# A semaphore increment on GpSimd behind every row gather of a graph network kernel

## The chip, the cores and the metric

The kernel runs on one core of one Trainium2 chip, as one launch of a hand-scheduled program with five instruction streams. The metric is device time in microseconds (us); lower is better. Three runs of the kernel before gave 9662.51, 9666.22 and 9667.9 us.

## What is computed

The reference is a two-part graph network on 12,500 nodes of 96 features and 200,000 edges, sorted by destination (cut to what matters):

```
h = relu(layernorm(x))                       # x: (12500, 96)
neigh1 = segment_sum(h[src], dst) * inv_deg
neigh2 = segment_sum(neigh1[src], dst) * inv_deg
x = x + 0.5 * neigh1 + 0.5 * neigh2
h = relu(layernorm(x))
for W_msg, W_edge, W_root, b in layer 1, layer 2:
    msg = h[src] @ W_msg + edge_attr @ W_edge            # (200000, 96)
    h = leaky_relu(max over the edges of a node (msg) + h @ W_root + b)
return x + h
```

So four times, one after the other, a row of 96 floats is fetched for each of the 200,000 edges and folded into the rows of the destination nodes: twice as a sum, twice as a maximum.

## The kernel before, in words

**Rounds.** The program has four rounds (`ROUNDS`, r = 0 to 3). In a round GpSimd gathers the rows of table r from HBM for all edges; rounds 0 and 1 sum (`sums`), rounds 2 and 3 take maxima (`maxima`). After the gathers a node stage works through the nodes in 14 chunks (`CHUNKS`) and writes the next table, and the next round's gathers wait until that table is stored (`tstored`, line 367).

**Groups.** 512 edges (4 columns of 128) are a group; there are 391 groups (`GROUPS`) a round. A group takes four gathers, one for each column: `pool.indirect_dma_start` at line 374 fetches 128 rows of 384 bytes, one for each partition, and its DMA adds 16 to the semaphore `landed` of the group's slot. That is 1564 gathers a round and 6256 in all. The rows go into `rows`, a ring of 8 group slots (`RING`). Before the first gather of group g, from the ninth group on, GpSimd waits until TensorE has used the slot: `pool.wait_ge(used, g - RING + 1)`, where `used` is `picked` in the sum rounds and `rows_ps` in the maximum rounds. Both are counters that TensorE increments with its last matmul of a group. GpSimd's program is written out in full; nothing else stands between the gathers of a round.

**Who uses the rows.** In the sum rounds TensorE multiplies the rows of a group with one-hot matrices (line 557, 8 matmul instructions a group) and increments `picked`; VectorE waits for `picked`, adds the windows into `comp` (line 784) and builds the next one-hots (lines 767 and 773); ScalarE waits for `picked` too in round 0 (line 435). TensorE waits for VectorE's folding of the group before the last one. In the maximum rounds TensorE adds the edge features and the rows in PSUM (lines 576 and 578) and increments `rows_ps`; VectorE scans (line 799); TensorE transposes the running maximum (line 589); ScalarE copies it (line 443); TensorE picks the segment ends (line 600) and ScalarE copies windows into `comp` (line 452). The edge features and the flags come by DMAs from SyncE's queue.

**The node stage on GpSimd.** Behind the gathers of a round GpSimd waits for the last folding and then builds some one-hots (line 388). Ahead of each chunk's one-hots it already has a semaphore increment of its own, `pool.sem_inc(pool_go, 1)` at line 386. No engine waits for `pool_go`.

Of the kernel before, what the change touches and what calls it, by code (L numbers as in the profile page):

```python
# [74 lines left out]
def after(q, n):  # L75

    return q >= n if known(q) else True


def pipeline(engine, body, lag):  # L80

    first = 2 + lag + (2 + lag) % 2
    pairs = (CHUNKS - first - 1) // 2
    for k in range(first):
        body(k, k % 2)
    with engine.Fori(0, pairs) as i:
        for s in range(2):
            body(i * 2 + (first + s), s)  # L90
    for k in range(first + 2 * pairs, CHUNKS + lag):
        body(k, k % 2)


def has(k, lag):

    return 0 <= k - lag < CHUNKS if known(k) else True


def gnn(nc, x, srcs, cur, prev, nxt, cur_r, prev_r, eat, wm1, we1, wr1, b1, wm2, we2, wr2, b2, out):  # L100
    with ExitStack() as ctx:
# [3 lines left out]
        def sem(name):  # L105
            return ctx.enter_context(nc.semaphore(name))
# [104 lines left out]
        pool_go, dve_go = sem("pool_goes_on"), sem("dve_goes_on")  # L211
# [132 lines left out]
        @block.gpsimd  # L344
        def _(pool):
            pool.memset(ident[:], 0.0).then_inc(const, 1)
            pool.memset(ident_b[:], 0.0).then_inc(const, 1)
            pool.memset(upto_b[:], 1.0).then_inc(const, 1)
            pool.memset(ones_b[:], 1.0).then_inc(const, 1)
            pool.wait_ge(const, 4)  # L350
            for eye in (ident, ident_b):
                pool.affine_select(out=eye[:], in_=eye[:], compare_op=ALU.not_equal, fill=1.0, base=0,
                                   pattern=[[-1, P]], channel_multiplier=1).then_inc(const, 1)
            pool.affine_select(out=upto_b[:], in_=upto_b[:], compare_op=ALU.is_ge, fill=0.0, base=0,
                               pattern=[[1, P]], channel_multiplier=-1).then_inc(const, 1)
            pool.wait_ge(const, 7)
            pool.affine_select(out=upto_b[:], in_=upto_b[:], compare_op=ALU.is_gt, fill=0.0, base=0,
                               pattern=[[0, P]], channel_multiplier=1).then_inc(const, 1)
            for to, w, step, first in ((iota_0, P, 1, 0), (iota_1, P, 1, 1), (iota_b, P, 1, 0), (tile_at, TILES, P, 0)):
                pool.iota(to[:], pattern=[[step, w]], base=first, channel_multiplier=0,  # L360
                          allow_small_or_imprecise_dtypes=True).then_inc(const, 1)
            pool.memset(comp[:], 0.0).then_inc(cleared, 1)

            pool.wait_ge(s_src, 16)
            for r in range(ROUNDS):
                for s in range(2):
                    pool.wait_ge(tstored[r][s], 16 * (CHUNKS // 2))
                used = picked[r] if r in sums else rows_ps[r]
                for g in range(GROUPS):
                    if g >= RING:  # L370
                        pool.wait_ge(used, g - RING + 1)
                    for j in range(GRP):
                        c = g * GRP + j
                        pool.indirect_dma_start(rows[:, g % RING, j, 0:D], None, tables[r][:, :],  # L374
                                                bass.IndirectOffsetOnAxis(src_sb[:, c:c + 1], 0)
                                                ).then_inc(landed[r][g % RING], 16)

                pool.wait_ge(folded[r], COLS)

                def spread(k, s):  # L380
                    if not has(k, 0):
                        return
                    pool.wait_ge(rel_ready[r], k + 1)
                    if after(k, 2):
                        pool.wait_ge(spread_ps[r], k - 1)
                    pool.sem_inc(pool_go, 1)
                    for j in range(POOL_HOTS[r]):
                        pool.tensor_scalar(spread_c[:, s, j, :], iota_1[:, :], rel_c[:, s, j:j + 1],  # L388
                                           None, ALU.is_equal).then_inc(spread_1h[r], 1)

                pipeline(pool, spread, 0)
# [587 lines left out]
```

## Time and profile before

| | |
|---|---|
| runs of the kernel before | 9662.51, 9666.22, 9667.9 us (median 9666.22) |
| the profiled execution's own time | 9629.93 us |
| its span, first to last instruction | 9628.2 us |
| GpSimd (POOL) busy | 6458.6 us, 67% of the span |
| of it the 6256 gathers | 6273.4 us |
| TensorE busy | 5576.1 us, 58% |
| VectorE busy | 3262.5 us, 34% |
| mean granted clock of TensorE | 0.648 of 2.4 GHz |
| DMA | 548.56 MB, mean 57 GB/s |

The profile is of one execution, which took 9629.93 us; the median of the runs lies 36.3 us above it. POOL is GpSimd, PE is TensorE's matmuls and PEld its weight loads, DVE is VectorE, ACT is ScalarE. A letter q behind an engine's name is its sequencer: instructions that only touch registers or semaphores. Those aren't counted as busy, and lists of instructions leave them out; the chain of waits shows them. "issue" is time in which an engine waited for nothing that the profile shows, "remote" a wait for a semaphore whose update could not be tied to an instruction.

### The profile page before, as it was taken

The page shows a single profiled execution, that of the slowest core. Times are in us where ns is not written, and L with a number is a line of the kernel's source. Part 1 is how long each engine was busy: PE and PEld are TensorE (multiplying, and loading weights), DVE is VectorE, ACT ScalarE, POOL GpSimd, SP SyncE. Part 2 cuts the span into 40 slices and gives each one's busy share as a digit, 9 for nine tenths or more (in the row PEclk, how much of TensorE's full clock was granted, in tenths as well). Part 3 has the DMA queues.
Part 4 walks back from the last instruction along what each step waited for, and adds up shares of the span by engine and source line. Part 5 has one row for each costly group of instructions (what it writes and reads, how often), then busy time and mean ns, then how long its engine had stood idle before and what let it go on. Part 6 is the DMA issues. An engine that isn't in the chain of part 4 may idle for free.

```text
span 9628.2 us, 100471 instructions
## 1 busy us (share of the span) xinstructions
PE 5576.1 (58%) x25651; PEld 4095.6 (43%) x25651; DVE 3262.5 (34%) x6693; ACT 1500.7 (16%) x5073; POOL 6458.6 (67%) x6525
## 2 busy tenths in 40 slices
PE   2333333334233333333578877878887887887888
PEld 1222222223222222222555555555564555555556
DVE  4333333334333232323423333333332333333334
ACT  1000000001000000000322222222232222222223
POOL 5666666664666666666566666766656666666665
PEclk6555555556555555555767777777786777677776
DMA  3111111111111111111133333333323333333332
GB/s 79 35 34 34 34 34 34 34 35 39 47 35 34 34 34 35 34 34 35 46 76 77 77 77 77 78 80 78 77 64 71 80 78 77 77 77 77 77 81 64
DMA packets 309643, 548.56 MB, mean 57 GB/s; under 512 B 183464, under 2 KB 183464, under 8 KB 284712
## 3 DMA queue, kind: packets, MB, share of 16 engines
q0 software_dynamic: 200192, 307.90, 16.3%
q1 hardware_dynamic: 108804, 239.50, 9.7%
q14 instruction: 77, 0.63, 0.0%
q8 instruction: 22, 0.36, 0.0%
q10 hardware_dynamic: 548, 0.17, 0.0%
HBM read 522.27 MB, written 24.87 MB: 57 GB/s over the span
## 4 chain that ended last, share of the span: by engine, by line
another core or an unknown queue 29%; PE 26%; issue 9%; DVE 8%; DVEq 2%; ACT 1%; ACTq 1%; POOL 0%; DMA 0%; POOLq 0%; SPq 0%
PE ps L578 7%; PE ps L576 6%; PE ps L600 6%; PE ps L589 3%; DVE arena L799 3%; DVE comp L784 3%; PE ps L557 2%; DVE arena L767 2%; DVEq L257 1%; DVEq L784 1%; PE ps L662 1%; PE ps L638 0%; ACTq L257 0%; PE ps L675 0%
## 5 line engine op out<-in xcount | busy, mean ns | idle before, releaser
L374 POOL DMA_INDIRECT rows<-table,src_sb x6256 | 6273.4, 1003 | 2930.3 <-issue 1767.5
L557 PE MATMUL ps<-arena,rows 128*98 128x128 f32 (+1 forms) x6256 | 1418.1, 399 | 2967.0 <-DVE comp L784 2634.6
L557 PEld LDWEIGHTS ps<-arena,rows 128*98 128x98 f32 (+1 forms) x6256 | 1179.5, 254 | 3226.7 <-DVE comp L784 2836.3
L799 DVE TENSOR_TENSOR_SCAN arena<-arena,ps 96x512 f32<-96x512 f32 x782 | 996.6, 1274 | 3238.6 <-remote 1989.8
L784 DVE TENSOR_TENSOR comp<-comp,ps 98x128 f32 (+1 forms) x3128 | 893.6, 286 | 2878.4 <-remote 2317.0
L578 PEld LDWEIGHTS ps<-ident,rows 128*96 128x96 f32 x6256 | 950.4, 208 | 912.9 <-issue 912.7
L600 PE MATMUL ps<-arena 128*96 128x128 f32 x6256 | 1180.2, 352 | 108.6 <-issue 72.4
L578 PE MATMUL ps<-ident,rows 128*96 128x128 f32 x6256 | 1173.3, 344 | 54.2 <-issue 53.4
L576 PE MATMUL ps<-arena,we 32*96 32x512 f32 x1564 | 1143.7, 819 | 27.3 <-DMA rows<-table,src_sb 27.3
L600 PEld LDWEIGHTS ps<-arena 128*96 128x96 f32 x6256 | 1052.2, 228 | 129.6 <-issue 124.4
L767 DVE TENSOR_TENSOR arena<-iota_b,meta 128x512 f32<-128x512 bf16 x1564 | 1053.0, 673 | 59.6 <-issue 55.1
L452 ACT COPY comp<-ps 96x128 f32 x3128 | 821.3, 263 | 1490.8 <-PE ps L600 573.6
L589 PE MATMUL ps<-ident,arena 96*128 96x96 f32 x3128 | 564.2, 322 | 757.8 <-DVE arena L799 653.8
L589 PEld LDWEIGHTS ps<-ident,arena 96*128 96x128 f32 x3128 | 449.1, 190 | 831.0 <-DVE arena L799 657.9
L443 ACT COPY arena<-ps 128x384 f32<-128x384 f32 x782 | 374.5, 479 | 1998.1 <-remote 1233.2
L435 ACT COPY rows<-root 128x4 f32 (+1 forms) x391 | 74.3, 197 | 2179.0 <-remote 1581.1
L492 ACT COPY rel_c<-node_rel 128x7 f32<-128x7 f32 (+1 forms) x42 | 8.5, 203 | 2261.8 <-DVE comp L784 2261.8
L388 POOL TENSOR_SCALAR arena<-iota,rel_c 128x128 f32<-128x128 f32 x252 | 172.0, 698 | 228.4 <-ACT rel_c L492 134.0
L576 PEld LDWEIGHTS ps<-arena,we 32*96 32x96 f32 x1564 | 236.2, 196 | 186.9 <-issue 125.4
L773 DVE TENSOR_TENSOR arena<-iota_b,meta 128x392 bf16<-128x392 bf16 x391 | 219.5, 561 | 12.0 <-issue 11.6
L563 PE MATMUL ps<-arena,ones_b 128*1 128x392 bf16 x391 | 168.3, 430 | 0.0
L662 PE MATMUL ps<-arena 128*128 128x96 f32 (+1 forms) x784 | 141.1, 354 | 6.4 <-ACT arena L504 4.8
(84 smaller groups left out, 1026.0 us busy)
## 6 DMA issues: line engine op xcount, KB each, us to landing
arena<-flags SPq DMA_DIRECT2D x194, 768.0 KB
rows<-table,src_sb POOLq DMA_INDIRECT x6256
arena<-in_eat SPq DMA_DIRECT2D x194, 256.0 KB
table<-arena SPq DMA_DIRECT2D x56, 336.0 KB, 2.7
out<-xs SPq DMA_DIRECT2D x13, 336.0 KB
xs<-in_x SPq DMA_DIRECT2D x6, 672.0 KB, 5.9
arena<-flags SPq DMA_DIRECT2D x2, 576.0 KB
src_sb<-in_srcs SPq DMA_DIRECT2D x1, 782.0 KB, 5.2
```

The costliest lines, as they stand in the source:

```text
L374: pool.indirect_dma_start(rows[:, g % RING, j, 0:D], None, tables[r][:, :], bass.IndirectOffsetOnAxis(src_sb[:, c:c + 1], 0)).then_inc(lan ...
L443: act.copy(runT[:, slot % SCANS].rearrange("p k d -> p (k d)"), ps[:, RUNT + slot % 2 * BANK:RUNT + slot % 2 * BANK + GRP * D]).then_inc(r ...
L452: act.copy(comp[0:D, bass.ds(at, P)], ps[0:D, WIN + slot % 2 * BANK + j * P:WIN + slot % 2 * BANK + (j + 1) * P]).then_inc(folded[r], 1)
L557: m = pe.matmul(ps[0:w, at + k * P:at + (k + 1) * P], rows[:, j, k, 0:w], hot[:, j % HOTS, k, :], start=True, stop=True)
L576: pe.matmul(ps[0:D, at:at + W], we[D:P, r - 2, :], fe[D:P, u, q * W:(q + 1) * W], start=True, stop=False)
L578: m = pe.matmul(ps[0:D, at + k * P:at + (k + 1) * P], rows[:, slot, k, 0:D], ident[:, :], start=False, stop=(k == GRP - 1))
L589: m = pe.transpose(ps[:, at:at + D], run[:, slot % SCANS, k * P:(k + 1) * P], ident[0:D, 0:D])
L600: m = pe.matmul(ps[0:D, at:at + P], runT[:, slot % SCANS, k, :], hot[:, slot % HOTS, k, :], start=True, stop=True)
L662: m = pe.matmul(ps[:, at_spread + j * P:at_spread + j * P + w], spread_c[:, qs, j, :], win_c[:, qs, j, 0:w], start=True, stop=True)
L767: dve.tensor_tensor(hot[:, slot % HOTS], ids, rel, ALU.is_equal).then_inc(hot_ready[r], 1)
L784: dve.tensor_tensor(win, win, ps[0:w, of:of + P], ALU.add).then_inc(folded[r], 1)
L799: dve.tensor_tensor_scan(run[:, slot % SCANS], fe[0:D, slot // UNIT, q * W:(q + 1) * W], ps[0:D, ROWS + slot % 2 * BANK:ROWS + slot % 2 * ...
```

## The change

One line is added, inside the loop over the four gathers of a group: GpSimd increments the semaphore `pool_go` by one behind each gather. No engine waits for it, no gather waits for it, and nothing else is moved. It is executed 6256 times.

```diff
@@ -374,6 +374,7 @@
                         pool.indirect_dma_start(rows[:, g % RING, j, 0:D], None, tables[r][:, :],
                                                 bass.IndirectOffsetOnAxis(src_sb[:, c:c + 1], 0)
                                                 ).then_inc(landed[r][g % RING], 16)
+                        pool.sem_inc(pool_go, 1)
 
                 pool.wait_ge(folded[r], COLS)
```

## Rows read from the trace of the kernel before

**Rows 1.** The page's busy times of the engines (part 1).
```profile
PE 5576.1 (58%) x25651; PEld 4095.6 (43%) x25651; DVE 3262.5 (34%) x6693; ACT 1500.7 (16%) x5073; POOL 6458.6 (67%) x6525
```
**Rows 2.** The page's group of the gathers: busy, mean ns | idle before, releaser.
```profile
L374 POOL DMA_INDIRECT rows<-table,src_sb x6256 | 6273.4, 1003 | 2930.3 <-issue 1767.5
```
**Rows 3.** All gathers by source line: shortest, median and longest duration in ns.
```profile
L374 POOL DMA_INDIRECT rows<-table,src_sb x6256: 942/947/2477, 61.0 to 9521.9; - x196
```
**Rows 4.** Waits: engine and line <- waited for: us in total, times, longest.
```profile
DVE comp L784 <- remote: 2317.0, 306, 20.8
...
DVE arena L799 <- remote: 1989.8, 283, 12.4
...
POOL rows L374 <- issue: 1767.5, 5787, 1.6
...
POOL rows L374 <- remote: 1008.3, 422, 5.8
...
POOL rows L374 <- DMA table<-arena: 91.4, 4, 46.9
```
**Rows 5.** POOL's timeline, round 0: both ends of 20 gathers [idle before].
```profile
2004.96 0.95 POOL L374 DMA_INDIRECT rows<-table,src_sb  x1 [3.08 <-remote]
...
2033.85 0.94 POOL L374 DMA_INDIRECT rows<-table,src_sb  x1 [3.35 <-remote]
```
**Rows 6.** Gathers by windows, pause to pause: length, busy (count), PEclk, DMA share, GB/s.
```profile
1618.95:1647.79 28.84, 19.29 (x20) 0.50 0.16 34
...
425.92:454.82 28.90, 20.00 (x20) 0.62 0.16 34
...
3736.20:3782.07 45.87, 31.58 (x32) 0.57 0.16 34
3415.30:3461.18 45.88, 32.36 (x32) 0.57 0.17 34
6241.21:6264.92 23.71, 16.24 (x16) 0.72 0.33 77
5915.75:5939.45 23.70, 16.96 (x16) 0.72 0.38 78
```
**Rows 7.** Gathers by windows, 2000 us each, of round 0 and of round 2.
```profile
200.00:2200.00 2000.00, 1354.31 (x1387) 0.59 0.16 34
...
4900.00:6900.00 2000.00, 1386.27 (x1352) 0.71 0.35 77
```
**Rows 8.** Timeline of round 0, twelfth group's matmuls and what followed.
```profile
132.46 2.02 PE L557 MATMUL ps<-arena,rows 128*98 128x128 f32 x8 [3.07 <-DMA rows<-table,src_sb]
...
165.24 0.94 POOL L374 DMA_INDIRECT rows<-table,src_sb  x1 [0.31 <-issue]
...
170.47 0.95 POOL L374 DMA_INDIRECT rows<-table,src_sb  x1 [4.29 <-remote]
171.17 1.55 DVE L784 TENSOR_TENSOR comp<-comp,ps 98x128 f32 x4 [20.82 <-remote]
```
**Rows 9.** Timeline of round 2, one group's matmuls and what followed.
```profile
6013.21 1.11 PE L578 MATMUL ps<-ident,rows 128*96 128x128 f32 x8
6013.74 0.95 POOL L374 DMA_INDIRECT rows<-table,src_sb  x1 [0.30 <-issue]
...
6016.35 1.27 DVE L799 TENSOR_TENSOR_SCAN arena<-arena,ps 96x512 f32<-96x512 f32 x1 [7.83 <-remote]
6016.43 0.95 POOL L374 DMA_INDIRECT rows<-table,src_sb  x1 [1.74 <-remote]
```
**Rows 10.** Chain of waits in the node stage around line 386: start, us, what.
```profile
4705.72 0.04 issue
4705.76 0.02 POOLq L386
4705.78 0.15 issue
```
**Rows 11.** Chain of waits at the start of round 1: line 367 and first gather.
```profile
2412.10 0.02 POOLq L367
2412.91 1.46 POOL rows L374
```

## The prediction

> **What bounds the kernel now.** I read the page's busy times first [rows 1]. No engine is full: POOL is busy 67% of the span, PE 58%. The gathers are 6273.4 us of POOL's 6458.6, and POOL idles 2930.3 us just before gathers [rows 2], so from its first gather to its last POOL does nearly nothing else: 6273.4 + 2930.3 = 9203.7 of the 9628.2 us. The rounds are bound by the pace of the gathers, and the question is what sets that pace.
>
> The pace has two parts. A plain gather lasts 0.947 us [rows 3] and is followed by a gap of 1767.5 / 5787 = 0.305 us that nothing is waited for in [rows 4]: 1.252 us each. On top come pauses: 1008.3 us of "remote" waits [rows 4], where POOL stands ahead of the first gather of a group and waits for TensorE's counter. Counted whole, the idle time less the four waits for a table and less a plain gap for every gather is 2930.3 - 91.4 - 6252 x 0.305 = 932 us of pauses [rows 2, 4]. In round 0 one comes after 20 gathers, 3.08 and 3.35 us long, 28.89 us apart [rows 5].
>
> Why does POOL wait, when TensorE is idle too? In round 0 TensorE ends the matmuls of the twelfth group at 132.46 + 2.02 = 134.48. VectorE, which waits for that increment, folds at 171.17, and POOL, which waits for the same increment, goes on at 170.47, having stopped at 166.18 [rows 8]. In round 2 the matmuls end at 6014.32, POOL stops at 6014.69, and VectorE and POOL start within 0.1 us of each other at 6016.35 and 6016.43 [rows 9]. So TensorE's increments become visible late, often only once POOL has stopped for a while; 2317.0 and 1989.8 us of VectorE's waits have the same mark [rows 4]. I can't see what holds them.
>
> I can see how long. Two stretches of 20 gathers, from a pause's end to the next one's, last 28.84 and 28.90 us although the gathers in them are busy 19.29 and 20.00 us: where gathers ran 0.71 us longer, the pause was 0.65 us shorter. The same holds for 32 gathers (45.87 and 45.88 us, busy 31.58 and 32.36) and for 16 in round 2 (23.71 and 23.70, busy 16.24 and 16.96) [rows 6]. It looks like a debt: each gather puts about 28.87 / 20 = 1.44 us of work on something, takes 1.25 to 1.3 us itself, and the pause pays the rest. Over 2000 us the pace is 2000 / 1387 = 1.442 us in round 0 and 2000 / 1352 = 1.479 us in round 2 [rows 7]. I take these as the real pace, and the pauses as its other half.
>
> **The change, part by part.** It adds 6256 increments by POOL's sequencer. Nobody waits for the semaphore and no DMA is added. What is queued behind each is the next gather.
>
> The price of one. The nearest row is the same instruction at line 386: 0.02 us, with 0.04 us of issue ahead of it [rows 10]; 0.06 us if POOL's sequencer comes to it only once the gather is done. The low end is 0: it passes while a gather runs. The high end is what an increment costs ahead of an idle engine, 0.04 + 0.02 + 0.15 = 0.21 us [rows 10]; further out, the first gather of round 1 starts 0.81 us after such an instruction [rows 11], but that gather also waits for a table. I take 0.06, because gathers follow each other at a constant 0.305 and so seem to be handled one by one.
>
> The sum. POOL's own pace becomes 1.252 + 0.06 = 1.312 us, plus what gathers run over: 1354.31 / 1387 - 0.947 = 0.029 us in the sum rounds and 1386.27 / 1352 - 0.947 = 0.078 in the maximum rounds [rows 3, 7]. That is 1.341 against a pace of 1.442, and 1.390 against 1.479. There is still slack, 0.101 and 0.089 us a gather, so the added 6256 x 0.06 = 375 us come out of the 932 us of pauses, which fall to some 557, and the rounds take as long as before. The cover is the pauses; if it were gone, the 375 us would be paid. Even the first high end, 0.21, would exceed the slack by only 0.049 and 0.061 us a gather: 3128 x 0.110 = 344 us. A small gain is likelier than a small loss, since fewer pauses leave fewer stretches in which the engines restart one after another; I put 16 us on it. Against the profiled execution that is 9628 - 16 = 9612 us of span and 9614 of its own time; the median of the runs is 36 us above it, so **9650 us**. 0.2% of 9666 is 19 us, about what a measurement of this kernel tells from no change.
>
> **The rivals.**
> *Nothing is spaced* (chance 0.10). POOL's sequencer runs through the increment while a gather is busy, and the profile after is the one before: 9666 us. For it: an increment is no work of the engine itself. Against: the constant 0.305 us, which looks like a sequencer that handles gathers one by one [rows 4]. The Trainium skill says in "Advanced Engine Details and Errata", section Sequencer Loop, that control instructions run in the sequencer while engine instructions are queued; by that rule the price would be 0 and this rival holds. No row of this trace shows an increment beside a running gather.
>
> *The increments get through* (0.20). The debt is an illusion of averages; what holds TensorE's counter is that gathers follow each other too closely, and a slightly longer gap is enough. Then the ring is freed in time, the pauses go, and POOL pays only the price: 932 - 375 = 557 us less, 9666 - 557 = 9109 us. For it: in rows 9 everything is released 1.6 us after POOL stops, not by anything TensorE did. Against: the equal stretches of [rows 6]. It decides if, with a gap of 0.37 us, VectorE's start follows TensorE's end by well under 1 us. [...]
>
> *Every gap is paid, slower* (0.18). A pause is a fixed time that POOL must stand still once the ring is full, and not a debt. Then 20 gathers take 20 x 0.06 = 1.2 us longer and the pause stays: 9666 + 375 = 10041 us. For it: the pauses are alike in length, 3.08 and 3.35 us [rows 5]. Against: [rows 6], where longer gathers shortened them. It decides from the point where the stretch of 20 gathers grows past 28.9 us.
>
> *The gap is long, slower* (0.08). The increment makes the sequencer start each gather from rest, at 0.21 us up to 0.81 us each. At 0.21 it costs the 344 us worked out above, 10010 us; at 0.81 the pace would be about 2.1 us and the kernel a third slower. For it is only [rows 11].
>
> **How the numbers follow.** The forecast, absorbed spacing, has 0.44: of it 0.22 within 0.2%, 0.16 faster by some tenths of a per cent (shorter restarts, a shorter tail of a round), 0.06 slower. With the rivals: faster 0.16 + 0.20 = 0.36; within 0.2% 0.22 + 0.10 = 0.32; slower 0.06 + 0.18 + 0.08 = 0.32. The forecast's own range is 9560 to 9730. The whole range goes down to the rival on the fast side, 9109, and up to half of the slow one, 9860: 0.44 + 0.10 + 0.20 + about 0.07 = 0.81 of the chance.
>
> **What would show it.** In the profile after: the plain gap between gathers 0.36 to 0.38 us instead of 0.305; the gathers' mean unchanged at 1.00 us; the pace over 2000 us still 1.44 and 1.48 us; stretches of 20 gathers still 28.9 us, with pauses of about 2 instead of 3.2 us; "remote" waits of POOL near 600 us. A gap still at 0.305 means that nothing is spaced. A pace of 1.34 with no pauses, and VectorE starting within 1 us of TensorE, means that the increments get through. Stretches of 30 us with pauses of 3 us mean that the gap is paid, and a gap above 0.5 us that the increment starts each gather from rest. I am wrong if the pace in rounds 0 and 1 moves by more than 1% either way.

## The result: slower by 0.5%, and the profile after

The kernel with the change takes 9711.65 us (median of 5 runs, 9709.59 to 9716.97), the kernel before beside it 9663.97 us. The ratio is 1.005, with a 95% interval of 1.0036 to 1.0065: 48 us slower. The forecast was 9650 us, a small gain. The profiled execution of the change took 9716.97 us.

The gathers of the page of the change (group: busy, mean ns, idle before), to compare with [rows 2], and its queues (packets, MB, share):

```profile
L374 POOL DMA_INDIRECT rows<-table,src_sb x6256 | 6227.7, 995 | 3050.4 <-issue 1782.5 <-remote 1126.3 <-DMA table<-arena 91.8
```
```profile
q14 instruction: 126, 1.03, 0.0%
q8 instruction: 22, 0.36, 0.0%
```

The gathers are no slower, rather quicker (995 against 1003 ns). All of the loss is idle time: 120 us more, nearly all of it "remote", 1126.3 against 1008.3 us. (The two profiled executions lie 87 us apart and the medians 48; the profiled one of before was 36 us below its median. So what these two profiles differ by is larger than what the change costs.) The second fence shows something the prediction had no term for: queue 14, which brings in instructions, moves 126 packets. Before it moved 77:

```profile
q14 instruction: 77, 0.63, 0.0%
```

Now the gap between two gathers. This is the chain of waits of the change at the start of round 1 (start, us, what):

```profile
2445.69 0.95 POOL rows L374
2446.64 0.02 issue
2446.66 0.02 POOLq L377
2446.68 0.26 issue
2446.94 0.95 POOL rows L374
```

The gap is 0.02 + 0.02 + 0.26 = 0.30 us, that of before [rows 4]. Over all, 1782.5 / 5738 = 0.311 us. Nothing is spaced.

The chain puts an increment (POOLq L377) between the two gathers, but it isn't the one that the program has there. There are 6256 increments and 6256 gathers, and counted off in order this increment is the 21st of the round, while the gather that has just ended is the ninth: POOL's sequencer is 12 gathers ahead. The same is seen from both ends of the program and in a short stretch. First a stretch of 2.8 us of the change, with six increments and three gathers; then all increments and all gathers of e18 below, which is the change on another chip (last two numbers ahead of the semicolon: first and last start):

```profile
L377 POOLq EVENT_SEMAPHORE  x6: 17/17/17, 1000.5 to 1003.1; - x6
L374 POOL DMA_INDIRECT rows<-table,src_sb x3: 945/983/984, 1000.6 to 1003.2; - x3
```
```profile
L377 POOLq EVENT_SEMAPHORE  x6256: 17/17/17, 62.6 to 8407.3; - x196
L374 POOL DMA_INDIRECT rows<-table,src_sb x6256: 940/944/2475, 62.8 to 8421.4; - x196
```

The last increment stands behind the last gather in the program, and it starts 14.1 us before that gather does. Every one of the 6256 increments starts before its own gather, in the change between 1 and 12 gathers ahead, half of the time at least 4. So the sequencer hands gathers over to be done later and runs its increments meanwhile, some of them while a gather is busy. The gap of 0.30 us is the engine's own, and the increments take no part in it.

Still the pace is slower. The gathers by windows of 2000 us, then by stretches from pause to pause (length, busy (count), PEclk, DMA share, GB/s), to compare with [rows 6, 7]:

```profile
200.00:2200.00 2000.00, 1338.48 (x1375) 0.58 0.16 34
4900.00:6900.00 2000.00, 1364.96 (x1341) 0.72 0.35 77
```
```profile
1199.58:1222.88 23.30, 15.16 (x16) 0.50 0.16 34
1530.84:1559.90 29.06, 20.31 (x20) 0.62 0.16 34
1031.25:1060.25 29.00, 19.47 (x20) 0.56 0.16 34
```

2000 / 1375 = 1.455 us in round 0 and 2000 / 1341 = 1.491 us in round 2, against 1.442 and 1.479: 0.012 us more for each gather, 6256 x 0.012 = 75 us of the 87 us that lie between the two spans (by the medians, 48 / 6256 = 0.008 us). The debt is still a debt (the stretches of 20 last 29.00 and 29.06 us although their busy times differ by 0.84 us), but it has grown by a hair: 29.0 instead of 28.9 us for 20 gathers, and 23.30 for 16 where the kernel before has

```profile
402.94:425.92 22.98, 15.28 (x16) 0.57 0.17 34
```

One part of the growth seems to be seen directly. In the change, 21 gathers that open no group, and so wait for nothing, start 1.3 to 1.8 us late, within a round always a multiple of 88 gathers apart; before there is none. One of them on POOL's timeline:

```profile
228.99 1.11 POOL L374 DMA_INDIRECT rows<-table,src_sb  x1 [1.75 <-issue]
```

88 gathers with their increments are 176 instructions, so I took the jumps for places where POOL runs out of fetched instructions (the loop kernels below contradict that). They add up to some 28 us. From here there were two theories: **F**, the doubled program has to be fetched, and **I**, each increment (or instruction) adds to the debt by itself. And the absorption, on which the forecast rested, was untested, because nothing had been spaced.

### The profile page after: what moved, and what is told of

It reads as the page before. It is cut to its first block, busy times and chain, and to the rows that moved or that the text cites. A ratio compares the mean times of both kernels' runs of the same rounds, so it can differ in the third digit from the quotient of the medians.

```text
span 9715.2 us, 106727 instructions
## 1 busy us (share of the span) xinstructions
PE 5627.5 (58%) x25651; PEld 4138.2 (43%) x25651; DVE 3267.3 (34%) x6693; ACT 1498.8 (15%) x5073; POOL 6412.4 (66%) x6525
## 4 chain that ended last, share of the span: by engine, by line
another core or an unknown queue 33%; PE 24%; issue 12%; DVE 10%; DVEq 5%; ACT 1%; ACTq 1%; POOL 0%; DMA 0%; POOLq 0%; SPq 0%
PE ps L579 7%; PE ps L577 6%; PE ps L601 6%; DVE comp L785 4%; DVE arena L768 3%; PE ps L590 3%; DVE arena L800 3%; DVEq L257 2%; DVEq L785 1%; PE ps L558 1%; ACTq L257 1%; PE ps L639 1%; PE ps L663 0%; DVE arena L774 0%
## 5 line engine op out<-in xcount | busy, mean ns | idle before, releaser
L374 POOL DMA_INDIRECT rows<-table,src_sb x6256 | 6227.7, 995 | 3050.4 <-issue 1782.5
L558 PE MATMUL ps<-arena,rows 128*98 128x128 f32 (+1 forms) x6256 | 1469.1, 410 | 2949.7 <-DVE comp L785 2551.3
L558 PEld LDWEIGHTS ps<-arena,rows 128*98 128x98 f32 (+1 forms) x6256 | 1223.7, 263 | 3216.0 <-DVE comp L785 2744.6
```

Source lines behind the costliest of these rows:

```text
L558: m = pe.matmul(ps[0:w, at + k * P:at + (k + 1) * P], rows[:, j, k, 0:w], hot[:, j % HOTS, k, :], start=True, stop=True)
```

## The experiments

Each kernel was timed beside the kernel before, on the same chip. They came to five chips, and the kernel before took 9556 us on that of e1 to e4, 9635 on that of e5 to e8, 9629 on that of e9 to e12, 8510 on that of e13 to e16 and 8523 on that of e17 and e18. The last two groups turn out to matter.

### What is added: a no-op, fewer and more increments, a hidden memset

e1 puts a no-op in the increment's place, e2 one increment behind each group, e3 three behind each gather. (Here and below only the lines that matter are shown; tiles, semaphores and closing waits that go with them are left out.)

```
                                                ).then_inc(landed[r][g % RING], 16)
+                        pool.nop()                        # e1
+                        if j == GRP - 1:                  # e2
+                            pool.sem_inc(pool_go, 1)
+                        for _ in range(3):                # e3
+                            pool.sem_inc(pool_go, 1)
```

> A no-op of the sequencer stands where the change has its increment: as many instructions (2 per gather), no increment. Theory F (fetching: POOL's program of gathers is twice as long, and its instructions are brought in by DMA twice as often, 126 against 77 packets in the profile of the change) expects the time of the change, 9712 us or 1.005 of the kernel before, with the same jumps of 1.3 to 1.8 us between gathers and about 126 packets. Theory I (the increments themselves: each adds about 0.012 us to what the gathers owe before TensorE's counter comes through) expects 9664 us, a ratio within 0.001 of 1, though with the packets of the change.

> One increment behind the fourth gather of every group instead of one behind each: a quarter of the added instructions and a quarter of the increments. Both theories F and I are linear in what is added and expect a quarter of the 48 us, 9676 us (ratio 1.0013). A rival, that any increment between groups costs by its place (it stands right ahead of the wait for TensorE's counter), expects most of the 48 us again, about 9700.

> Three increments behind each gather. If the cost is linear in instructions or increments (F and I alike): 3 x 48 = 144 us, 9808 us (ratio 1.015). If the 0.305 us between two gathers is long enough to hide them all, the plain gap stays at 0.305; if the increments take 0.02 to 0.06 us each and only the first is hidden, the gap grows to 0.35 to 0.43 us. Fetching by F: about 77 + 3 x 49 = 224 packets on the queue that fetches instructions.

e1: ratio 0.9993 (0.9979 to 1.0008), but queue 14 moves 77 packets as before. The compiled program has no instruction for the no-op, so e1 is the kernel before once more and decides nothing. It shows only how well two equal kernels agree. e2: 1.0000 (0.9985 to 1.0014) with 90 packets, which excludes that one increment ahead of the wait costs all; a quarter of 0.5% can't be told from nothing. e3: 1.0078 (1.0051 to 1.0105) with 224 packets; 75 us by the ratio and 85 by the medians, not the 144 of three times the change. Its gap:

```profile
999.79 0.94 POOL L374 DMA_INDIRECT rows<-table,src_sb  x1 [0.30 <-issue]
1001.04 0.98 POOL L374 DMA_INDIRECT rows<-table,src_sb  x1 [0.30 <-issue]
1002.33 0.94 POOL L374 DMA_INDIRECT rows<-table,src_sb  x1 [0.31 <-issue]
```

Even three increments leave the 0.30 us as it was.

e4 puts work of the engine there instead:

```
+                        z = pool.memset(spacer[:, c % 64 * 2:c % 64 * 2 + 2], 0.0)
+                        if c % 32 == 31:
+                            z.then_inc(spaced[r], 1)
+                            if c > 31:
+                                pool.wait_ge(spaced[r], c // 32)
```

> Real work of the engine instead of an increment: a memset of 128x2 bf16 behind each gather (with one increment and one wait in 32 of them, which is met long before), so the gathers are really spaced. Left out: nothing of what is computed. The memset takes perhaps 0.06 to 0.2 us, and the distance of two gathers grows by that. Theory D of the prediction (a debt of 1.44 us a gather that pauses pay off, so that spacing below 0.1 us a gather is absorbed) expects the 9712 us of the change or a little more when the spacing is 0.1 us or less, and for a spacing s above 0.1 us about 9712 + 6256 x (s - 0.1): 10340 us at 0.2. The rival, that a pause is a fixed time and every gap is paid, expects 9712 + 6256 x s: 10340 us at 0.1 and 10960 us at 0.2. The rival, that spaced gathers let TensorE's increments through, expects the pauses (1008 us of remote waits before) to go to near 0.

POOL's timeline in e4:

```profile
1000.59 0.94 POOL L377 DMA_INDIRECT rows<-table,src_sb  x1 [0.19 <-issue]
1001.54 0.11 POOL L380 MEMSET spacer<- 128x2 bf16 x1
1001.84 0.95 POOL L377 DMA_INDIRECT rows<-table,src_sb  x1 [0.19 <-issue]
```

A memset of 0.11 us and 0.19 us of issue make the same 0.30, and the gathers follow each other in 1.25 us as ever. So e4 didn't space them either. But it cost 1.0041 (1.0026 to 1.0056), as much as the change, with 128 packets and one increment in 32 gathers. So increments aren't needed for the cost: about as many added instructions of another kind cost about as much.

### Gathers that are really spaced

e6, e7 and e9 to e12 have a memset wide enough to outlast the gap; e5 is the change again beside them.

```
+                        n = r * COLS + c
+                        if n:
+                            pool.wait_ge(spaced, n)
+                        pool.memset(spacer[:, 0:300], 0.0).then_inc(spaced, 1)
```

> The change itself once more, beside the other kernels of this call, because the first four runs were made on a chip where the kernel before takes 9556 us instead of 9664. Theory F (what costs is that POOL's program of gathers is twice as long and has to be fetched; the memset of e4, which lay inside the 0.305 us between gathers, cost 0.4% with 128 packets of instructions): 1.004 to 1.005 of the kernel before, the plain gap at 0.305, 126 packets. A rival, that the 0.5% belonged to one chip: within 0.002 of 1.

> A memset of 128x300 bf16 behind each gather, with an increment that the next memset waits for. The memset of 128x2 took 0.117 us of the 0.305 and that of comp 10651 ns for 12672 columns, 0.84 ns a column, so this one should take 0.117 + 298 x 0.00084 = 0.37 us and be 0.06 us longer than the gap: distance of plain gathers 1.31 instead of 1.252 us if the gather starts right behind it (1.50 if the 0.19 us of issue come again behind the memset). This is the spacing the prediction had counted on. Theory D (a debt of some 1.43 us a gather, paid by pauses): 6256 x 0.06 = 375 us come out of the pauses, the time stays within 0.6% of the kernel before (that is, 0.4% for the fetching and little else), and remote waits fall by some 300 us. Rival P (a pause is a fixed time, every gap is paid): 375 us on top, ratio 1.044. Rival G (spaced gathers let TensorE's increments through): remote waits near 0, ratio 0.95 to 0.98. At a distance of 1.50 us D expects 1.50 x 6256 and no pauses, ratio about 1.06.

> The same with 128x420 bf16: by the same rate 0.47 us, so the distance of plain gathers becomes 1.252 + 0.16 = 1.41 us. Theory D: 1.41 + 0.03 (sum rounds) and 1.41 + 0.08 (maximum rounds) against a pace of 1.43 and 1.46: the cover is just used up; pauses nearly gone, ratio 1.005 to 1.02. Rival P: 6256 x 0.16 = 1000 us, ratio 1.10. Rival G: the pace is 1.44, remote waits near 0, ratio 1.005 to 1.02 as well; D and G are told apart by e6, not here.

e5: 1.0048 (1.0034 to 1.0062), 126 packets; the cost belongs to the change. e6: 1.0327 (1.0313 to 1.0341). e7: 1.0942 (1.0927 to 1.0957). In both the 0.16 us of issue come again behind the memset, so the distance of e6 is not 1.31 but 0.945 + 0.365 + 0.16 = 1.47 us, above the debt's 1.44. Its timeline in round 0:

```profile
1000.76 2.02 PE L564 MATMUL ps<-arena,rows 128*98 128x128 f32 x8 [4.05 <-DMA rows<-table,src_sb]
1000.96 0.94 POOL L377 DMA_INDIRECT rows<-table,src_sb  x1 [0.16 <-issue]
1001.89 0.37 POOL L383 MEMSET spacer<- 128x300 bf16 x1
1002.43 0.95 POOL L377 DMA_INDIRECT rows<-table,src_sb  x1 [0.16 <-issue]
...
1002.90 0.20 ACT L442 COPY rows<-root 128x4 f32 x1 [6.28 <-PE ps L564]
...
1003.40 1.55 DVE L791 TENSOR_TENSOR comp<-comp,ps 98x128 f32 x4 [3.85 <-PE ps L564]
```

TensorE ends at 1002.78, ScalarE goes on at 1002.90, VectorE at 1003.40, and POOL never stops. In [rows 8] VectorE had to wait for 20.82 us. Of POOL's remote waits one of 0.2 us is left. That fits a debt that is now always paid, and as well a rule that spaced gathers let the increments through. The distances between 1.25 and 1.44 us had to decide.

> The kernel of e6 with a narrower memset, 128x60 bf16. By the rate that e4, e6 and e7 show (0.117, 0.365 and 0.465 us for 2, 300 and 420 columns, with 0.16 to 0.19 us of issue behind it) it takes about 0.165 us and the distance of plain gathers is about 1.28 us instead of 1.252. Theory D (debt): pauses fall by 6256 x 0.03 = 190 us and the time is that of e4, 1.004 of the kernel before. P (pauses fixed): 1.004 + 0.02 = 1.024. G (increments get through once the gathers are spaced): remote waits gone, ratio about 0.93, if the threshold lies below 1.28.

> Memset of 128x100 bf16: about 0.2 us, distance about 1.31 us, the spacing the prediction had counted on. D: ratio 1.004 to 1.01, remote waits of POOL near 600 us, pace 1.43 and 1.46. P: 1.004 + 6256 x 0.06 / 9635 = 1.043. G: 1.31 + 0.03 and 1.31 + 0.08 us a gather and no remote waits, ratio about 0.95.

> Memset of 128x160 bf16: about 0.25 us, distance about 1.36 us. D: ratio 1.004 to 1.01, remote waits of POOL below 300 us. P: 1.075. G: no remote waits, ratio about 0.975.

> Memset of 128x220 bf16: about 0.3 us, distance about 1.41 us. D: ratio 1.005 to 1.015, remote waits of POOL below 100 us. P: 1.10. G: no remote waits, ratio 1.00 to 1.01; so G and D differ only in the three narrower ones.

The sum of POOL's remote waits in each, from the waits of e9, e10, e11 and e12 (us in total, times, longest):

```profile
POOL rows L377 <- remote: 849.1, 385, 4.2
```
```profile
POOL rows L377 <- remote: 628.1, 326, 4.5
```
```profile
POOL rows L377 <- remote: 343.6, 223, 3.1
```
```profile
POOL rows L377 <- remote: 82.0, 71, 1.7
```

| kernel | memset, us | distance, us | remote waits, us | ratio (95%) |
|---|---|---|---|---|
| e4 | 0.117 | 1.25 | 903 | 1.0041 (1.0026 to 1.0056) |
| e9 | 0.165 | 1.27 | 849 | 1.0037 (1.0024 to 1.0051) |
| e10 | 0.198 | 1.31 | 628 | 1.0052 (1.0038 to 1.0066) |
| e11 | 0.248 | 1.35 | 344 | 1.0062 (1.0048 to 1.0075) |
| e12 | 0.298 | 1.40 | 82 | 1.0089 (1.0076 to 1.0103) |
| e6 | 0.365 | 1.47 | 0.2 | 1.0327 (1.0313 to 1.0341) |
| e7 | 0.465 | 1.57 | 0 | 1.0942 (1.0927 to 1.0957) |

(The distance is the mean memset plus 0.945 us of a plain gather and 0.16 us of issue; for e4 and e10 it is what plain gathers show on the timeline.) From e4 to e11 the gathers move apart by 0.1 us, 626 us in all, and the time grows by 0.2%. The remote waits give 559 us of it back. From e6 to e7, past 1.44 us, another 0.1 us costs 596 us of the 626 that it adds, 6%: it is paid nearly in full. Two stretches of 20 gathers of e10:

```profile
435.67:464.61 28.94, 19.19 (x20) 0.62 0.17 34
1205.32:1234.42 29.10, 19.82 (x20) 0.62 0.16 34
```

The same 29 us, with POOL doing 20 x 0.055 = 1.1 us more of its own. The debt behaves as forecast on these chips, spacing is absorbed, and neither "every gap is paid" nor "the increments get through" survives: at 1.31 us the one expected 1.043, the other 0.95, and 1.0052 was measured.

### Gathers in a loop

e8 takes the fetching within a round away: 32 gathers stand in a loop, and their row numbers are copied to a small table first.

```
+                        pool.tensor_copy(idx[:, 16 * h:16 * h + 4 * m],
+                                         src_sb[:, bass.ds(i * (RING * GRP) + 16 * h, 4 * m)]).then_inc(indexed[r], 1)
+                        pool.wait_ge(indexed[r], i * 2 + (h + 1))
...
+                            pool.sem_inc(pool_go, 1)
...
+                                                        bass.IndirectOffsetOnAxis(idx[:, k * GRP + j:k * GRP + j + 1], 0)
...
+                sweeps(pool, gather)
```

> The gathers in a hardware loop of 32 (8 groups) instead of 6256 written out, so that their instructions needn't be fetched anew. For that the row numbers are copied, 16 columns at a time, from the static table to a small one by a POOL copy of 128x16 (0.2 to 0.3 us with its wait, per 16 gathers), and the copy waits until the gathers that read the same columns before have landed. One increment per group holds the wait for TensorE's counter. Theory F expects the packets on the instruction queue to fall from 77 to under 40, the jumps of 1.3 to 1.8 us to go, and the time at or below the kernel before: fetching of 77 packets at the price of the added 49 (0.4%) is worth up to 0.6%, ratio 0.994 to 1.0 with the copies absorbed by the pauses. A rival, that fetching costs nothing and the pace is set by the gathers alone: 1.000. A second one, that the branch of the loop and the copies are paid in full (0.3 us x 2 + 1 us, 196 times): 314 us, ratio 1.03.

34 packets, and 1.0184 (1.017 to 1.0198). The copy is dear on POOL's timeline:

```profile
1067.32 0.94 POOL L385 DMA_INDIRECT rows<-table,idx  x1 [0.30 <-issue]
1068.28 0.20 POOL L377 COPY idx<-src_sb 128x16 uint32 x1
1069.34 0.96 POOL L385 DMA_INDIRECT rows<-table,idx  x1 [0.86 <-issue]
```

0.20 us of copy and 0.86 of idle time where a gap is 0.30, 392 times: 0.76 us each, 298 us, beside the loop's branch. The kernel is 177 us slower, so a part of it is absorbed. As a faster kernel the loop fails.

It does settle what the jumps are not. Theory F expected them to go. But 42 gathers of e8 that open no group start 1.6 to 1.7 us late, at the same places as in the change (the 114th gather of a round, the 202nd, and on in steps of 88). One of them, and the only DMA queue that moved anything from 200 to 2300 us of e8:

```profile
359.04 0.94 POOL L385 DMA_INDIRECT rows<-table,idx  x1 [1.68 <-issue]
```
```profile
q0 software_dynamic: 45856, 70.53, 16.8%
```

In these 2100 us no packet of instructions came in, and the jumps are there. So they are not waits for fetched instructions. The increments show more, as they mark where the sequencer is. In the change and in e5 it takes 0.54 to 0.56 us from one increment to the next within a group, but 2.7 us at each of those places, also where no jump of POOL shows. With three increments a gather (e3) the stop comes every 88 gathers as well, though that is 352 instructions, and in e2, which has no jump, four gathers take it 4.1 us or more there and 1.9 elsewhere. Something stops the sequencer for 2.2 us every 88 gathers; POOL shows it only where it has few gathers left to do. What it is, and why it doesn't show in the kernel before, stays open.

The packets of instructions can be looked at directly too. From the end of one remote wait of over 1 us to the next, 12 gathers in rounds 2 and 3 of the change last 17.87 us (median of 139 stretches) without such a packet and 17.87 us (of 28) with one; in e3, with its 224 packets, 17.68 (63) and 17.70 us (63). Only a jump makes a stretch longer, 18.7 us in the change. Four such stretches of the change, the first and the third with a packet:

```profile
5446.85:5464.66 17.81, 12.21 (x13) 0.73 0.42 93
5464.66:5482.56 17.90, 12.52 (x12) 0.81 0.41 92
5542.47:5560.43 17.96, 12.34 (x13) 0.69 0.39 92
7021.67:7039.57 17.90, 12.27 (x13) 0.62 0.40 92
```

(The count takes in a gather that only touches the edge.) The kernel before has 17.76 us for such a stretch (113 of them), so most of the loss stands in stretches with neither a packet nor a jump. What is missing is the loop's twin, with an increment behind each gather (e13).

> The loop of e8 with an increment of POOL's own behind each gather, as in the change; its instructions are not fetched anew (34 packets in e8). Theory F (fetching costs the 0.5%) expects the time of the loop without the increments, within 0.15% of e14. Theory I (each further instruction or increment costs about 0.008 to 0.012 us by itself) expects 50 to 75 us more than e14, 0.5 to 0.8%.

> The kernel of e8 once more, beside e13 on the same chip: 1.018 of the kernel before, as measured.

e13: 1.0467 (1.0452 to 1.0481), e14: 1.0461 (1.0447 to 1.0475). The increments cost nothing that can be told from 0. But on this chip e14 is not at the 1.018 of e8, and the kernel before takes 8510 us. No engine shows a single remote wait in any of the four kernels profiled on this chip (e13 to e16). The copies and the branches are paid in full here, 387 us where e8 paid 177, because there are no pauses to absorb them. So these runs don't settle theory I: there was no debt for an increment to add to. The jumps are here as well, 36 in each of the two, on a chip without the debt, with 34 to 36 packets. One of e14, and its waits for issue:

```profile
220.01 0.95 POOL L385 DMA_INDIRECT rows<-table,idx  x1 [1.45 <-issue]
```
```profile
POOL rows L385 <- issue: 1824.4, 5824, 4.8
```

e15 and e16 halve what a gather brings: 48 columns of 128 rows, or 96 columns of 64 rows. Both leave out half of the gathered data.

```
-  pool.indirect_dma_start(rows[:, g % RING, j, 0:D], None, tables[r][:, :],
+  pool.indirect_dma_start(rows[:, g % RING, j, 0:D // 2], None,
+                          tables[r].rearrange("n (a d) -> (n a) d", a=2),          # e15
+  pool.indirect_dma_start(rows[0:P // 2, g % RING, j, 0:D], None, tables[r][:, :],   # e16
```

> Each gather brings 48 instead of 96 columns of a row, from a table seen as rows of 48; left out is half of what is gathered (the other columns hold ones). The rows, and so the descriptors, stay 128 a gather. If a gather's debt of 1.44 us is the writing or handling of its 128 descriptors, the pace stays at 1.43 to 1.48 us and the time within 1% of the kernel before. If it is the transfer of its 49 KB, the debt halves, the pauses go, and the pace is POOL's own 1.252 + 0.03 to 0.08 us: about 6256 x 0.15 = 940 us less, ratio 0.90.

> Each gather brings 64 instead of 128 rows, to half of the partitions; left out are the rows of the other half, which hold ones. If the debt is one of descriptors, it falls to about 0.72 us, and what is left is POOL's own time for a gather, which is not known for 64 rows: between 0.6 and 1.25 us. Pauses gone and no remote waits if the debt falls more than POOL's time does; pauses in the same share of the time, if both halve.

e15: 0.9975 (0.9966 to 0.9984); e16: 0.9718 (0.9703 to 0.9732). Their question, what the debt is made of, can't be answered on a chip without it. What they say of POOL: half the bytes leave a plain gather at 0.94 us, half the rows make it 0.90 us. POOL's time for a gather hardly depends on its bytes or its rows in this range.

### The change where there is no debt

> The loop with an increment behind each gather once more. On a chip with remote waits (before at 9550 to 9670 us), where the loop without increments took 1.0184 of before (e8): theory F (fetching) expects 1.017 to 1.020, theory I (each increment or further instruction costs 0.008 to 0.012 us by itself) expects 1.023 to 1.027. On a chip without them (before near 8510 us): 1.047, as in e13.

> The change itself. On a chip with remote waits: 1.005 once more. On a chip without them, where POOL goes at its own pace and the increment is hidden in the gap: by F only the jumps of the fetching are left, 21 of them with some 28 us in the profile of the change, ratio 1.003; by a rule that the whole 0.5% is a share of the debt, 1.000.

This chip, too, runs the kernel before in 8523 us and shows no remote wait. e17 repeats e13: 1.0457 (1.0443 to 1.0472). e18, the change: **0.9997 (0.9988 to 1.0006)**. Its queues, waits of POOL and windows:

```profile
q14 instruction: 126, 1.03, 0.0%
```
```profile
POOL rows L374 <- issue: 1891.5, 6207, 0.3
POOL arena L389 <- ACT rel_c L493: 95.5, 30, 13.5
POOL rows L374 <- DMA table<-arena: 92.9, 4, 48.8
```
```profile
200.00:2200.00 2000.00, 1460.30 (x1482) 0.51 0.19 40
4600.00:6600.00 2000.00, 1446.83 (x1458) 0.80 0.39 86
```

The same program and the same 126 packets, but the longest wait for issue is 0.3 us instead of 1.8: no jump shows. The sequencer is 12 gathers ahead here nearly all of the time, some 15 us, so a stop of 2.2 us would not reach POOL (argued, not shown). The pace is 2000 / 1482 = 1.350 us in round 0 and 2000 / 1458 = 1.372 us in a maximum round. Here POOL itself is the bound (1.252 us and what gathers run over), and the doubled program is free. TensorE's clock isn't what differs: the 11 runs of the change on this chip take 8510 to 8527 us with a granted clock from 0.656 to 0.780.

## Why the prediction was wrong

**The bound and the debt: right, on this chip.** Equal stretches with unequal busy time were the right thing to read. e9 to e12 confirm the debt, the slack and its end: spacing is absorbed up to 1.40 us and paid beyond 1.44.

**Absorbed spacing: right as a mechanism, and not what the change does.** The forecast said that the pauses would fall to 557 us. e10 has the spacing that it meant, and 628 us of remote waits. In the change they rose.

**The price of an increment, 0.06 us: wrong.** For the gap it is 0. The step that failed reads "gathers follow each other at a constant 0.305 and so seem to be handled one by one". By POOL they are, by its sequencer they aren't: that is up to 12 gathers ahead, and its increments run beside the gathers. The rival "nothing is spaced", given 0.10, holds for the gap, and for the reason that it gave; its time, 9666 us, lies some 46 us too low. The Trainium skill says in "Advanced Engine Details and Errata", section Sequencer Loop, that control instructions run in the sequencer while engine instructions are queued. By that rule the price was 0, and the trace agrees: the last increment of e18 starts 14.1 us before the last gather. Work of the engine itself is another matter: a memset of 0.117 us fits into the gap unseen, one of 0.165 us no longer does (e4, e9).

**"The rounds take as long as before": the step that failed for the sign.** The sum let the added instructions take their 0.06 us from the pauses and put at nothing, without a reason, what they might add to the debt itself. The term is 48 / 6256 = 0.008 us a gather by the medians; in the two profiles the pace went from 1.442 to 1.455 us and from 1.479 to 1.491. e4 costs as much without an increment behind each gather, and e2, with a quarter of the increments, nothing that can be measured. And e18 shows that even this cost needs a chip that has the debt. "No DMA is added" was wrong as well, 49 packets of instructions are, and 90, 126, 128 and 224 packets go with 1.0000, 1.0048, 1.0041 and 1.0078; but added instructions and packets grow together, and stretches with a packet are no longer than those without. I had put 16 us of gain on shorter pauses; no spaced kernel gained anything.

That 9712 us lies within the range of 9560 to 9730 is owed to the width of the range: the 375 us that were to be absorbed were never spent, and the 48 us that were lost were in no term.

**The rivals.** "The increments get through" and "every gap is paid" fell with e10. The Trainium skill warns in "VectorE: DVE Perf Modes", section on the TRN2 errata of SBUF-source operations, that semaphore increments at a high rate from one engine can deadlock another. It speaks of a deadlock and not of increments that come late, and no run here stops for good. TensorE's increments come late already in the kernel before, where POOL's sequencer has no increment between the gathers and only their DMAs increment. "The gap is long" fell with the gap of 0.30 us; its price for 0.81 us was also worked out wrongly, as 0.947 + 0.81 us is a pace of about 1.8 us, not 2.1.

**What stays open.** Why an added instruction costs 0.008 us a gather on a chip with the debt. Its fetching is spoken against: the jumps, up to 28 of some 75 us (in e5 28 of them with 35 us, in e4 10 with 15 us), come without any fetching in the loop, e9 and e10 have 126 packets, no jump and cost 0.4 and 0.5%, and packets make no stretch longer. What is left is that each further instruction adds to the debt in some way (theory I), and no run isolates that: the twin loops that should have told it ran where nothing costs anything. Open, too, are the sequencer's stop every 88 gathers and what the debt is.

No version beat both kernels. The loop and every spaced kernel are slower than before on the chips with the debt.

## What to carry to other kernels

An idle time between two instructions of one engine, equal thousands of times, is not proof that the sequencer is busy in it: compare where the sequencer's own instructions start with where the engine's do. When a change adds instructions to a long unrolled program, count the packets of the instruction queue, but compare stretches with and without a packet before you blame them. And before a mechanism is built on late semaphores, run the unchanged kernel on a second chip: what bounds it on one may not exist on the next.

## What the runs showed of the hardware

- The kernel before takes (medians) 9556 to 9664 us in the first runs and on three chips of the experiments, and 8510 and 8523 us on two others, with the granted clock alike (0.646 in the profile of the change, 0.657 in that of e18). On the slower ones TensorE's increments become visible late while POOL issues gathers faster than one per 1.44 us (1.48 in the maximum rounds); on the two faster ones they come at once.
- Where they come late, spacing the gathers to 1.47 us makes them prompt (remote waits in e6: 0.2 us of POOL, 25.8 of VectorE, 98.1 of ScalarE, against 1008, 4307 and 3312 us in the kernel before) but costs more than the waiting.
- A gather of 128 rows keeps POOL for 0.94 us and the next follows after 0.30 us, in which 0.117 us of memset pass unseen. 128 rows of half the width take as long, 64 rows 0.90 us.
- POOL's sequencer runs up to 12 gathers ahead of POOL. One or three increments a gather run there, each some 0.08 us of the sequencer's time (0.54 us a gather with one, 0.69 with three), and leave the gap at 0.30 us.
- Every 88 gathers the sequencer stops for 2.2 us, unrolled or in a loop, with one or three increments a gather, on both kinds of chip; POOL then shows a jump of 1.3 to 1.9 us if it has few gathers left to do.
- 49 further packets of instructions cost nothing where POOL is the bound (0.9997), and stretches of gathers with a packet last as long as those without (17.87 and 17.87 us).
